# Four products of a constant tile on TensorE ahead of the first load, in a two-layer decoder kernel

## The chip, the cores and the metric

The kernel runs on one core of a Trainium2 chip. The metric is the time of one execution on the device in microseconds (us); lower is better. The inputs, weights and outputs are float32 and lie in the chip's memory; the core loads all of them itself at the start of each execution.

## The reference

The reference is a decoder with two layers over x of shape (8, 128, 128): 8 batches, 128 tokens, 128 channels. Each of six sub-blocks is added to its input and layer-normalised:

```
x = norm(x + gated_delta_rule(x))          # 16 heads of 8 channels, a scan over the tokens
x = norm(x + cross_attention(x, ctx))      # strided keys, 16 heads
x = norm(x + quantum_ffn(x))               # 128 -> 512 -> 128, with a sine in between
x = norm(x + selective_scan(x))            # 256 inner channels, 16 states, a scan over the tokens
x = norm(x + perceiver_attention(ctx, x))  # 8 heads of 128, keys from ctx and x
x = norm(x + receptance_ffn(x))
```

Only the head of the first sub-block matters for what follows. It is a projection and what hangs on it:

```
qkv   = x @ Wqkv.T                 # queries, keys, values
q, k  = q / |q|, k / |k|           # per head of 8 channels
alpha = sigmoid(x @ Wg.T + bg); beta = sigmoid(x @ Wb.T + bb)
S_t   = alpha (S - beta (S k) k') + beta v k'   # then o_t = S_t q_t
```

## The kernel before, in words

The kernel is one program written out by hand for the five engines. Each engine (TensorE, VectorE, ScalarE, GpSimd, and SyncE, which issues the DMAs) has its own block of instructions, runs them in the order in which they are written, and waits on named semaphores where it needs another engine's result. No scheduler moves anything. The output buffer of TensorE is one tile `ps` of eight banks with 512 columns each; `bank(k)` is the k-th.

SyncE issues eight loads right at the start (L374 to L381). The first, half of the pack `first`, holds the weights of the first projection, the gate biases and the first four batches of x, transposed; it raises `first_in`. The second holds the other four batches and the identity matrix and raises `second_in`. The context, the weights of later blocks and, last, the pack `late` (L381) follow.

TensorE begins with a wait for `first_in` (L1611). Then it multiplies each of the 8 batches with the weights of queries, keys, values and gates at once, 416 columns, into banks 0 to 7 (L1615). Each such float32 product is two weight loads and two matmuls in the trace, so L1615 stands there with 16 of each. ScalarE copies the even banks into the arena (L1174) and squares the queries and keys (L1170), VectorE copies the odd banks (L471) and squares the last batch (L477). TensorE then turns the gates (L1620), turns and sums the squares (L1628), and turns keys, queries and values (L1633). ScalarE applies the sigmoid (L1187) and the square root (L1190), VectorE the reciprocal (L501), and from there VectorE forms the small triangular systems and runs the scan over 32 chunks of 4 tokens (L566 to L581), with GpSimd and ScalarE beside it.

In later stages TensorE runs some products that nothing reads. The helper `stay_awake(n, k)` (L1597 to L1602) issues n products of the identity with 256 columns of the first weights into bank k. It can't be used before the first load has landed, since its operands come with that load.

ScalarE copies a small matrix out of the pack `late` (L1201) before it goes on with the folded weights of the second cross attention (L1204).

Of the kernel before, what the change touches and what calls it, by code (L numbers as in the profile page):

```python
# [18 lines left out]
P = 128  # L19
B, T, D = 8, 128, 128  # L20
# [62 lines left out]
def decoder(nc, first, x, early, context, fold, late, rows, out):  # L83
    with ExitStack() as ctx:
        sems = {}

        def S(name):
            name = RIDES[name][0] if name in RIDES else name
            if name not in sems:
                sems[name] = ctx.enter_context(nc.semaphore(name))  # L90
            return sems[name]
# [5 lines left out]
        def sb(name, shape, dt=F32):  # L97
            return ctx.enter_context(nc.sbuf_tensor(name, shape, dt))
# [40 lines left out]
        lat_mean = sb("lat_mean", [P, HB])  # L139
        cmean_rstd = sb("cmean_rstd", [P, B])  # L140
        table = sb("table", [P, 1])
        neg_a = sb("neg_a", [P, NH, NS])
        arena = sb("arena", [P, 27000])
        ps = ctx.enter_context(nc.psum_tensor("ps", [P, 8 * BANK], F32))
# [42 lines left out]
        def bank(k, n=1):  # L187
            return ps[:, k * BANK:(k + n) * BANK]
# [208 lines left out]
        def _(ve):  # L397
            count = [0]

            def step(ins):  # L400

                count[0] += 1
                ins.then_inc(S("vector_step"), 1)
# [62 lines left out]
                ve.wait_ge(S("normed"), normed(n, batches[-1] + 1))  # L466


            for b in range(1, B, 2):
                ve.wait_ge(S("qkv_mm"), b + 1)  # L470
                nc.vector.tensor_copy(qkvt[:, :, b], bank(b)[:, 0:3 * D + 2 * H].rearrange("p (n h) -> p n h", h=H)).then_inc(S("qkv_odd"), 1)  # L471
                if b == B - 3:
                    ve.wait_ge(S("ctx_in"), 16)
                    for i in range(2):
                        step(nc.vector.bn_stats(cstats[0:TC, i], kv_ctx[0:TC, i]))
# [1117 lines left out]
        def _(pe):  # L1593
            mm, turn = nc.tensor.matmul, nc.tensor.transpose
# [13 lines left out]
                    turn(turned_bank(n, g)[:, b % HB * T:(b % HB + 1) * T], xrow[:, n % 2, b], ident).then_inc(S("turned"), 1)  # L1608


            pe.wait_ge(S("first_in"), 16)  # L1611
            for b in range(B):
                if b == HB:
# [10 lines left out]
            for n in range(2):  # L1624
                if n:
                    pe.wait_ge(S("gates"), 2)
                for j in range(DH):
                    ins = mm(norm2[n], sq[:, (1 - n) * DH + j].rearrange("p b h -> p (b h)"), ident, is_transpose=True,  # L1628
                             start=(j == 0), stop=(j == DH - 1))
# [34 lines left out]
            for c in range(0, NC - NTAIL, 4):  # L1664
# [8 lines left out]
                for n, (pr, terms) in enumerate(((prod_s, DH), (prod_a, C))):  # L1673
                    pe.wait_ge(S("prods"), 2 * (c + n_c - 1) + n + 1)
                    for j in range(terms):
                        ins = mm(bank(6 + c // NR)[:, at:at + n_c * C * DH], ident,  # L1676
                                 pr[:, j, c % NR:c % NR + n_c].rearrange("p c t i -> p (c t i)"),
                                 start=(n == 0 and j == 0), stop=(n == 1 and j == terms - 1))
# [131 lines left out]
            for m in range(2):  # L1810
                pe.wait_ge(S("xcol"), 5 + m)
                for n in range(NH):
                    ins = mm(bank(4 + n)[:, 2 * m * T:2 * (m + 1) * T], W("w_in")[:, n * P:(n + 1) * P], xcol[:, 2 * m:2 * m + 2],
                             start=True, stop=True)
# [173 lines left out]
            for q in range(NQ):  # L1988
# [61 lines left out]
                if NK4 - 1 <= q < NK4 + 3:  # L2050
                    for h in range(2 * (q - NK4 + 1), 2 * (q - NK4 + 2)):
                        mm(bank(7)[:, h:h + 1], fk[:, h], W("bq1")[:, h:h + 1], start=(h == 0), stop=False)
                        last = mm(bank(7)[:, D:2 * D], W("bv1")[:, h:h + 1].to_broadcast([P, P]), fo[:, h],
                                  start=False, stop=(h == XH - 1))
# [149 lines left out]
```

## Time and profile before

| | |
|---|---|
| time, median of 3 runs | 368.13 us (367.89 to 369.22) |
| span of the profiled execution, first to last instruction | 365.6 us |
| what lies around the span (median less span) | 2.5 us |
| TensorE busy (matmul) | 314.8 us, 86% |
| VectorE busy | 301.9 us, 83% |
| ScalarE busy | 222.6 us, 61% |
| GpSimd busy | 201.8 us, 55% |
| mean granted TensorE clock | 0.957 |
| TensorE's wait for the first load | 4.1 us, once |

The profiled execution's own time is not given apart from its span, so the median stands beside it. In the rows, PE is TensorE's matmul, PEld its weight load, DVE is VectorE, ACT is ScalarE, POOL is GpSimd and SPq the queue of SyncE. Busy time is the time in which an engine executes; the brackets at the end of a row in order of time tell how long the engine sat idle before it and what ended this. The granted clock is 1.00 at 2.4 GHz and 0.50 at 1.2 GHz.

### The profile page before, as it was taken

How to read it: one execution, taken by the hardware profiler on the slowest of the kernel's cores; microseconds unless marked ns; L12 is line 12 of the kernel's file. 1: busy time of each engine (PE TensorE's matmuls, PEld its weight loads, DVE VectorE, ACT ScalarE, POOL GpSimd, SP SyncE). 2: the span in 40 equal slices, each digit the busy share in tenths (PEclk: the TensorE clock that was granted, in tenths of full speed). 3: DMA queues.
4: the chain of work that ended last, by engine and by line, in shares of the span. 5: the costliest groups of instructions: out<-in, count | busy, mean ns of one | idle time of the engine just before them, and what ended most of it. 6: DMA issues, size and time to landing. Idle time of an engine off the chain costs nothing. (4 is left out here: it accounts for less than half of the span.)

```text
span 365.6 us, 5686 instructions
## 1 busy us (share of the span) xinstructions
PE 314.8 (86%) x1758; PEld 239.0 (65%) x1758; DVE 301.9 (83%) x746; ACT 222.6 (61%) x515; POOL 201.8 (55%) x240
## 2 busy tenths in 40 slices
PE   5949396898998999868869989898799989999993
PEld 2647295686765647734436965576698668989873
DVE  0798999997988899999999999999949434754945
ACT  4666233334265869897777638888565656765742
POOL 2399996765504051899999999969503700100111
PEclk9978599899999999999996999999999999999997
DMA  8910000000000003345544534534100000000011
GB/s 257 417 63 2 1 0 3 0 1 2 0 2 1 0 2 119 121 138 161 148 130 114 186 104 146 160 126 139 64 2 0 2 1 0 3 0 2 1 30 29
DMA packets 11525, 24.45 MB, mean 67 GB/s; under 512 B 1231, under 2 KB 2255, under 8 KB 11239
## 3 DMA queue, kind: packets, MB, share of 16 engines
q1 hardware_dynamic: 11495, 24.09, 20.2%
q8 instruction: 14, 0.23, 0.3%
q14 instruction: 16, 0.13, 0.1%
HBM read 23.50 MB, written 0.59 MB: 66 GB/s over the span
## 5 line engine op out<-in xcount | busy, mean ns | idle before, releaser
L1101 POOL TENSOR_TENSOR arena<-arena 128x512 f32<-128x512 f32 x63 | 80.0, 1280 | 22.7 <-DVE arena L746 21.2
L746 DVE TENSOR_TENSOR_SCAN arena<-arena,ps 128x512 f32<-128x512 f32 x64 | 77.2, 1208 | 0.1
L1387 ACT ACTIVATE arena<-arena,neg_a 128x508 f32<-128x508 f32 x64 | 44.0, 717 | 6.9 <-DVE arena L746 5.9
L1863 PE MATMUL ps<-first_in,arena 128*128 128x128 f32 x256 | 41.0, 284 | 3.9 <-POOL arena L1101 3.7
L739 DVE TENSOR_TENSOR ps<-arena,ps 128x512 f32<-128x512 f32 x64 | 43.1, 676 | 0.1
L1147 POOL TENSOR_TENSOR rstd<-veps,mhalf 128x4 f32<-128x4 f32 (+2 forms) x6 | 5.0, 838 | 67.5 <-DVE veps L848 35.5
L1863 PEld LDWEIGHTS ps<-first_in,arena 128*128 128x128 f32 x256 | 32.3, 146 | 14.9 <-POOL arena L1101 8.3
L774 DVE TENSOR_REDUCE arena<-ps 128x2 f32<-128x496 f32 x32 | 21.3, 667 | 24.8 <-PE ps L1909 24.8
L1847 PE MATMUL ps<-arena,pick_wide 96*128 96x512 bf16 x64 | 25.2, 399 | 11.8 <-DVE arena L746 11.4
L1676 PE MATMUL ps<-arena,first_in 128*128 128x128 f32 (+1 forms) x192 | 26.2, 299 | 9.4 <-POOL arena L971 9.4
L1250 ACT ACTIVATE arena<-arena 128x64 f32<-128x64 f32 x31 | 12.9, 415 | 33.4 <-DVE arena L581 33.4
L1676 PEld LDWEIGHTS ps<-arena,first_in 128*128 128x128 f32 x192 | 25.2, 213 | 12.2 <-POOL arena L971 12.1
L1437 ACT ACTIVATE first_in<-ps 128x256 f32<-128x256 f32 x32 | 12.4, 386 | 30.8 <-PE ps L1935 30.5
L1423 ACT ACTIVATE arena<-ps,arena 128x248 f32<-128x248 f32 x64 | 29.4, 472 | 0.0
L971 POOL TENSOR_TENSOR arena<-arena 128x256 f32<-128x256 f32 x32 | 23.7, 742 | 8.3 <-DVE arena L581 8.0
L1602 PE MATMUL ps<-first_in 128*128 128x256 f32 x102 | 26.2, 391 | 2.2 <-ACT arena L1219 2.2
L1847 PEld LDWEIGHTS ps<-arena,pick_wide 96*128 96x128 bf16 x64 | 6.3, 98 | 28.6 <-DVE arena L746 25.8
L1909 PE MATMUL ps<-kvT,arena 128*128 128x248 f32 x96 | 24.1, 374 | 0.0
L1602 PEld LDWEIGHTS ps<-first_in 128*128 128x128 f32 x102 | 18.7, 197 | 5.8 <-ACT arena L1219 2.6
L1431 ACT ACTIVATE arena<-ps 128x512 f32<-128x512 f32 x32 | 19.2, 600 | 1.5 <-PE ps L1923 0.4
L1946 PEld LDWEIGHTS ps<-fold_vo,first_in 128*128 128x128 f32 x128 | 18.4, 191 | 1.8 <-ACT first_in L1437 0.5
L986 POOL TENSOR_TENSOR rstd<-veps,mhalf 128x2 f32<-128x2 f32 x8 | 5.7, 708 | 25.0 <-DVE veps L422 24.8
(302 smaller groups left out, 808.8 us busy)
## 6 DMA issues: line engine op xcount, KB each, us to landing
arena<-c_rows_dram SPq DMA_DIRECT2D x64, 256.0 KB, 3.2
fold_in<-in_fold_dram SPq DMA_DIRECT2D x1, 2056.0 KB, 11.2
late_in<-in_late_dram SPq DMA_DIRECT2D x1, 1423.5 KB, 17.2
early_in<-in_early_dram SPq DMA_DIRECT2D x1, 921.5 KB, 13.0
xres<-in_x_dram SPq DMA_DIRECT2D x1, 512.0 KB, 13.8
kv_ctx<-in_context_dram SPq DMA_DIRECT2D x1, 480.0 KB, 7.0
first_in<-in_first_dram SPq DMA_DIRECT2D x1, 465.0 KB, 3.4
rows_in<-in_rows_dram SPq DMA_DIRECT2D x1, 384.0 KB, 14.3
```

Of the source, the lines that this page charges most:

```text
L739: tt(chain(q), dtu[:, n, cols(g)], chain(q), ALU.mult).then_inc(S("drive"), 1)
L746: nc.vector.tensor_tensor_scan(hist[:, q % NBUF], fade[:, q % NFADE], chain(q), 0.0, ALU.mult, ALU.add).then_inc(S("scan"), 1)
L774: nc.vector.tensor_reduce(s5_max[:, u % 2], sim, AX.X, ALU.max, negate=True).then_inc(S("sim_max"), 1)
L971: tt(prod_s[:, :, c % NR].rearrange("p j t i -> p t i j"), Qg[:, c].unsqueeze(2).to_broadcast([P, C, DH, DH]), state[:, c].unsqueeze(1).to ...
L1101: tt(seen[:, q % NBUF], hist[:, q % NBUF], c_wide[:, q % NBUF], ALU.mult).then_inc(S("read_out"), 1)
L1387: act(fade[:, q % NFADE].rearrange("p (b t) -> p b t", t=T)[:, :, 1:], dt[:, n, cols(g)].rearrange("p (b t) -> p b t", t=T)[:, :, 1:], ACT ...
L1423: act(s5_p[:, u % 2, h], sim_bank(u)[:, h * 256:h * 256 + KV], ACT.Exp, bias=s5_max[:, u % 2, h:h + 1], accum_out=s5_den[:, u % 2, h:h + 1 ...
L1602: mm(bank(k)[:, 0:256], ident, W("w_qkvgb")[:, 0:256], start=True, stop=True)
L1676: ins = mm(bank(6 + c // NR)[:, at:at + n_c * C * DH], ident, pr[:, j, c % NR:c % NR + n_c].rearrange("p c t i -> p (c t i)"), start=(n == ...
L1847: mm(chain(q), pick[:, s], bc_parts[0:96, cols(g)], start=True, stop=True).then_inc(S("b_mm"), 1)
L1863: ins = mm(y_bank(p // NS)[:, b * T:(b + 1) * T], seen[:, p % NBUF, b * T:(b + 1) * T], ident, is_transpose=True, start=False, stop=last a ...
L1909: ins = mm(sim_bank(u)[:, i * 256:i * 256 + KV], s5_q[b // HB][h + i][:, b % HB * T:(b % HB + 1) * T], kvT[:, b], start=True, stop=True)
```

## The change

A tile `warm` of 128 x 256 float32 is added. VectorE fills it with 0.5 as its first instruction and raises the semaphore `warm`. TensorE waits for that semaphore before its wait for `first_in`, and multiplies the first 128 columns of the tile with all of its 256 columns, four times, into the first 256 columns of bank 7. Bank 7 is next written by the projection of batch 7, which starts its sum anew, so nothing reads the four products.

```diff
@@ tiles @@
         table = sb("table", [P, 1])
+        warm = sb("warm", [P, 256])
         neg_a = sb("neg_a", [P, NH, NS])
@@ VectorE's block @@
+            nc.vector.memset(warm[:], 0.5).then_inc(S("warm"), 1)
             for b in range(1, B, 2):
                 ve.wait_ge(S("qkv_mm"), b + 1)
@@ TensorE's block @@
+            pe.wait_ge(S("warm"), 1)
+            for _ in range(4):
+                mm(bank(B - 1)[:, 0:256], warm[:, 0:P], warm[:], start=True, stop=True)
             pe.wait_ge(S("first_in"), 16)
             for b in range(B):
                 if b == HB:
```

On TensorE, at the head of the program, the order before is this; `first_in` is the first pack, `arena` the working tile, and a float32 product stands as one row.

```order
L1592 UNCONDITIONAL_BRANCH
L1615 MATMUL ps<-first_in 128x416 x8
L1620 MATMUL ps<-first_in,arena 128x128 x2
L1628 MATMUL ps<-first_in,arena 128x128 x16
L1633 MATMUL ps<-first_in,arena 128x128 x24
```

The same place after the change:

```order
L1594 UNCONDITIONAL_BRANCH
L1615 MATMUL ps<-warm 128x256 x4
L1620 MATMUL ps<-first_in 128x416 x8
L1625 MATMUL ps<-first_in,arena 128x128 x2
L1633 MATMUL ps<-first_in,arena 128x128 x16
L1638 MATMUL ps<-first_in,arena 128x128 x24
```

Four products stand ahead of the projection, which is now L1620; all else keeps its order. On VectorE, at the head of its block, before:

```order
L396 UNCONDITIONAL_BRANCH
L471 COPY arena<-ps 128x26x16 x3
L475 BN_STATS cstats<-kv_ctx 120x6 x2
L471 COPY arena<-ps 128x26x16
L477 TENSOR_TENSOR arena<-arena 128x16x16
```

and after the change:

```order
L397 UNCONDITIONAL_BRANCH
L470 MEMSET warm 128x256
L473 COPY arena<-ps 128x26x16 x3
L477 BN_STATS cstats<-kv_ctx 120x6 x2
L473 COPY arena<-ps 128x26x16
L479 TENSOR_TENSOR arena<-arena 128x16x16
```

The fill stands ahead of the first copy out of the projection. ScalarE, GpSimd and SyncE run what they ran.

## Rows read from the trace of the kernel before

**Rows 1.** The page, lines 2 and 4: 40 equal slices of the span; the last chain.

```profile
PEclk9978599899999999999996999999999999999997
...
PE 25%; DVE 1%; ACT 1%; issue 1%; POOL 1%; POOLq 0%; DVEq 0%
```

**Rows 2.** Instructions in time: start us, us, engine, instruction, idle before it.

```profile
0.73 1.28 ACT L1174 ACT_TABLE_LOAD   x1 [0.73 <-PEq L2193]
0.73 0.52 POOL L907 MEMSET arena<- 128x512 f32 x1 [0.29 <-POOLq L2193]
0.74 0.38 SPq L374 DMA_DIRECT2D first_in<-in_first_dram  x1
...
4.14 8.72 PE L1615 MATMUL ps<-first_in 128*128 128x416 f32 x16 [4.14 <-DMA first_in<-in_first_dram]
```

**Rows 3.** TensorE's weight loads of the first projection, same columns.

```profile
9.16 0.34 PEld L1615 LDWEIGHTS ps<-first_in 128*128 128x128 f32 x1 [0.36 <-issue]
9.85 0.24 PEld L1615 LDWEIGHTS ps<-first_in 128*128 128x128 f32 x1 [0.36 <-issue]
10.25 0.19 PEld L1615 LDWEIGHTS ps<-first_in 128*128 128x128 f32 x1 [0.16 <-issue]
```

**Rows 4.** Stretches: width, busy PE, PEld, DVE, ACT, POOL (count), PEclk, DMA share, GB/s.

```profile
5.00:6.00 1.00, 1.00 (x3) 0.64 (x2) 0.00 (x0) 0.06 (x1) 0.00 (x0) 1.00 1.33 340
...
23.00:24.00 1.00, 1.00 (x10) 1.00 (x9) 1.00 (x2) 1.00 (x1) 1.00 (x2) 0.80 0.00 0
```

**Rows 5.** Keep-awake products (L1602), at either clock level, in time.

```profile
38.05 2.07 PE L1602 MATMUL ps<-first_in 128*128 128x256 f32 x4 [2.15 <-ACT arena L1219]
...
48.54 1.03 PE L1602 MATMUL ps<-first_in 128*128 128x256 f32 x4
```

**Rows 6.** ScalarE, VectorE and TensorE around the first projection's end, in time.

```profile
5.94 0.52 ACT L1174 ACTIVATE arena<-ps 128x416 f32<-128x416 f32 x1 [3.92 <-PE ps L1615]
...
6.47 1.28 ACT L1159 ACT_TABLE_LOAD   x1
...
12.61 1.02 ACT L1170 ACTIVATE arena<-arena 128x256 f32<-128x256 f32 x3
12.90 0.59 DVE L471 COPY arena<-ps 128x416 f32<-128x416 f32 x1 [0.41 <-PE ps L1615]
13.53 0.42 DVE L477 TENSOR_TENSOR arena<-arena 128x256 f32<-128x256 f32 x1
...
14.08 0.63 ACT L1187 ACTIVATE arena<-ps,first_in 128x128 f32<-128x128 f32 x2 [0.45 <-PE ps L1620]
14.10 1.94 PE L1628 MATMUL ps<-first_in,arena 128*128 128x128 f32 x16
14.73 1.28 ACT L1190 ACT_TABLE_LOAD   x1
...
16.36 0.95 DVE L501 RECIPROCAL arena<-ps 128x128 f32<-128x128 f32 x1
```

**Rows 7.** The first load of constants for late stages, and ScalarE's use of it.

```profile
4.01 1.12 SPq L381 DMA_DIRECT2D late_in<-in_late_dram  x1
...
22.60 1.89 ACT L1201 ACTIVATE pick_wide<-late_in 96x2048 bf16<-96x2048 f32 x1
22.65 2.68 PE L1643 MATMUL ps<-fold_in 128*128 128x128 f32 x15 [4.00 <-DVE arena L512]
```

**Rows 8.** DMA issues of the page: size, us from issue to landing.

```profile
late_in<-in_late_dram SPq DMA_DIRECT2D x1, 1423.5 KB, 17.2
```

**Rows 9.** Later stretches; columns as in rows 4.

```profile
16.00:85.00 69.00, 52.47 (x309) 45.93 (x307) 67.20 (x272) 29.53 (x91) 58.39 (x82) 0.85 0.06 24
...
87.00:90.00 3.00, 1.96 (x16) 1.64 (x16) 1.36 (x4) 0.76 (x3) 1.22 (x6) 1.00 0.02 5
...
189.00:192.00 3.00, 2.02 (x10) 1.38 (x10) 3.00 (x5) 2.99 (x5) 2.88 (x3) 0.81 0.51 154
192.00:195.00 3.00, 2.50 (x10) 1.44 (x9) 3.00 (x5) 2.97 (x5) 2.67 (x3) 0.50 0.50 159
```

## The prediction

> **What bounds the kernel now.** I began with the page's clock line and its last chain [rows 1]. The chain is TensorE's in the last quarter of the span; before that it changes hands. The clock line has low digits in slices 3 to 5 and one in slice 22, and none in the first slice. The change is at the very start, so what counts is whether time won there reaches the end.
>
> Next I read the first microseconds in order of time [rows 2]. ScalarE, GpSimd and SyncE are let go at 0.73 to 0.74 us. TensorE does nothing until the first load lands at 4.14, so 3.4 us of it are free.
>
> Then I looked at how fast the projection ran. The clock column grants 1.00 at 5 to 6 us, and says 0.80 and less only from 23 us on [rows 4]. The durations say otherwise: a weight load takes 0.34 us at 9.16 and 0.19 at 10.25, and they stand 0.69 us apart (9.16 to 9.85) before the turn and 0.35 after it (the same 416 columns at twice the pace) [rows 3]. Before about 9.9 us TensorE ran at 1.2 GHz, after it at 2.4, and the column shows this only from its first recorded change on. The rise came 5.7 us after its first product (9.85 less 4.14). In the first 5.7 us eight of the 16 matmuls ran at half rate.
>
> The Trainium skill ("TensorE: Matmul & The Clock Gate", Part 1: The HAM clock gate) says that an idle array is held at 1.2 GHz by default and activity releases it. By that rule, the durations agree and the column does not.
>
> Who waits for the projection: VectorE and ScalarE stand idle for it, the last copy begins at 12.90 after 0.41 us of idling, and the turn of the gates, the sigmoid at 14.08, the table load at 14.73 and the reciprocal at 16.36 follow link by link [rows 6]. From 16 to 85 us VectorE is busy 67.20 of 69.00 us [rows 9]: the span there is its work, which starts when that chain lets it. So a shift at 16.36 moves the whole scan with it.
>
> **The change part by part.**
>
> *The fill.* No fill by VectorE stands in the trace. GpSimd fills 512 columns in 0.52 us [rows 2]; VectorE's product over 256 columns takes 0.42 [rows 6]. Bounds are 0.1 and 0.5 us; I take 0.3, nearest to half of the first. VectorE has nothing else to do then, so it costs nothing there. The step from VectorE to TensorE is 0.15 us (its last square ends at 13.53 + 0.42 = 13.95, TensorE begins at 14.10 [rows 6]). The block so begins at 0.74 + 0.3 + 0.15 = 1.2 us, between 1.0 and 1.4.
>
> *The four products.* They are 8 matmuls of 256 columns. At the low clock one takes 0.69 x 256/416 = 0.43 us, eight 3.4 us. The keep-awake products, which have this shape, agree on the ratio: four matmuls take 2.07 us at the low clock and 1.03 at the high one, tails and first load included [rows 5]. So the block ends at 1.2 + 3.4 = 4.6 us, 0.5 after the load has landed. It costs 0.5 us (between 0.3 and 0.7), unless the clock rises inside it.
>
> *The clock.* If it rises 5.7 us after the first product again, it rises at 6.9 us instead of 9.9. Projection before: 8.2 matmuls at 0.69 and 7.8 at 0.35, from 4.14 to about 12.6. Projection after, from 4.6: 2.3 us at the low clock are 3.3 matmuls, 12.7 follow at 0.35, that is 4.4 us, end at about 11.35. It ends 12.6 - 11.35, some 1.2 us earlier.
>
> *What is late next.* ScalarE: its first copy starts 1.80 us after the first matmul [rows 2, 6], so at 6.4. From there it has four copies of 0.52, a table load of 1.28 with 0.2 behind it, and seven squares of some 0.35 (1.02 for three): 6.0 us without a gap. It is through at 12.45, where it was through at 13.63 [rows 6]: 1.2 us earlier. VectorE's last square (13.95 before) comes at 12.7. TensorE's next stage starts behind the later of the two, at about 12.9 instead of 14.10. So 1.2 us are kept, and ScalarE has no slack left: any larger gain of TensorE would be cut to about what ScalarE lets through.
>
> *Loads.* `late` lands 17.2 us after its issue at 4.01, that is at 21.2 [rows 7, 8]. ScalarE uses it at 22.60, now at 21.4. It still does not wait, with 0.2 us to spare.
>
> *Sum.* 1.2 us off the profiled span of 365.6, so 364.4; with the 2.5 us between the span and the median of the runs, 366.9 us. As the profile is one execution and the runs differ by 1.3 us among themselves, I let the profiled execution stand for the median. Bounds of the unknown terms, start of the block and fill, move this by 0.2 us either way. Bounds of the rise are wider: not before 4.1 us (all of the projection at the high clock) and, at the latest, where it was.
>
> The same section of the Trainium skill says that the moment of the rise against the start of a kernel varies from run to run, and advises against fitting to one count of slow products. By that rule the 1.2 us are one draw among several; one profile can't show it here, so it goes into the spread only, and the middle stays at the row's 5.7 us.
>
> **The rivals.**
>
> *Nothing is won (368.0 to 368.4).* Either the rise stays at 9.9 us since these constants do not bring it on, or TensorE was at its high clock as the column says. In the first case the projection starts 0.5 us late and still meets the rise at 9.9: half of the 0.5 us is lost, +0.25, 368.4. In the second, the block takes 8 x 0.21 = 1.7 us, ends at 2.9 before the load, and the time is 368.1. For the second speaks only the column; against it the durations [rows 3, 4]. For the first speaks nothing but that no product of constants stands in the trace. A gain that a later wait swallows would give the same time; VectorE's 97% from 16 to 85 us speaks against it.
>
> *More than forecast (365.8).* The clock rises before or near the first load. Then the projection takes 16 x 0.35 = 5.6 us from 4.14 and ends at 9.8, 2.8 us earlier. ScalarE's 6.0 us from about 5.3 end at 11.3, 2.3 us earlier, and that is the cap: 365.8. Its table matrix would wait for `late` at 20.3 to 21.2, ahead of work that VectorE needs only at 32 us. Speaks for it: TensorE is active 2.9 us sooner; against it: the only rise measured at the start took 5.7 us of full work.
>
> *Slower (370).* Everything behind 16 us is moved against the moments at which the clock changes. The trace has it fall at about 191 us, when TensorE had been busy 2.02 of 3 us, and at 192 to 195 it stands at 0.50 [rows 9]. There VectorE was busy 3.00 of 3 and nothing was lost. At 87 to 90 us TensorE is busy only 1.96 of 3, VectorE and ScalarE even less, and the clock held at 1.00 [rows 9]. If it falls there in the moved timing, some 6 us of TensorE's work (one low slice or so, as at 192) run at half rate in a stage that waits for it: about +3 us, less the 1.2 won, 370. It decides from the point at which more than 2.4 us of such work lie on the path. In the profile all low stretches lie beside a busy VectorE, so this is a small chance.
>
> **How the numbers follow.** About 0.5% (1.8 us) is what a measurement of this kernel can tell from no change. Forecast: 366.9, 0.53. Nothing won: 0.23. More: 0.17. Slower: 0.07. The forecast itself lies within 0.5%. Faster by over 0.5%, below 366.3: three quarters of the third case and a sixth of the first, 0.22. Slower by over 0.5%, above 370.0: 0.05, as half of the last case and some spread. Same: 0.73. The range goes from the third case's time, less some, 365.5, to beyond the second's, 368.7. The forecast's own range is 366.2 to 367.6.
>
> **What would show it.** A fill on VectorE of 0.2 to 0.4 us at about 0.75; the first of 8 matmuls at about 1.2, half of them or more 0.43 us apart; the first weight load of 0.19 us near 7 us, where it was near 10; the reciprocal (16.36 before) near 15.2; and the same shift at 85 us and at the end. A rise at 9.9 shows the first rival, a projection all at 0.35 us the second. Wrong would be the forecast if the reciprocal moved by 1.2 us and the end did not, or if the block began after 2 us.

## The result: 365.06 us, 0.72% faster, outside the predicted range

| | median | lowest, highest | runs |
|---|---|---|---|
| before, beside it | 368.13 us | 367.89, 369.22 | 4 |
| changed | 365.06 us | 364.95, 365.21 | 4 |

The ratio is 0.9928, with a 95% interval of 0.9909 to 0.9946. The gain is 3.1 us in the medians, where 1.2 were forecast and the range ended at 365.5.

The page of the changed kernel, its clock line and its last chain, which answer to [rows 1]:

```profile
PEclk9968599899999999989987989999999999999997
...
PE 25%; DVE 1%; ACT 1%; issue 1%; POOL 1%; POOLq 0%; DVEq 0%
```

The chain is the same. The clock line has three more low digits in the middle (slices 18, 21 and 24, each at 8, beside slice 22); what one such stretch does is told below.

The head of the changed kernel in order of time (start us, us, engine, instruction, idle before it), answering to [rows 2, 3, 6, 7]:

```profile
0.86 0.27 DVE L470 MEMSET warm<- 128x256 f32 x1 [0.86 <-PEq L2198]
...
1.19 3.46 PE L1615 MATMUL ps<-warm 128*128 128x256 f32 x8 [1.19 <-DVE warm L470]
...
4.58 0.30 PEld L1620 LDWEIGHTS ps<-first_in 128*128 128x128 f32 x2 [0.34 <-DMA first_in<-in_first_dram]
4.58 5.85 PE L1620 MATMUL ps<-first_in 128*128 128x416 f32 x16
5.04 0.19 PEld L1620 LDWEIGHTS ps<-first_in 128*128 128x128 f32 x1 [0.16 <-issue]
...
10.19 1.02 ACT L1172 ACTIVATE arena<-arena 128x256 f32<-128x256 f32 x3
...
11.67 1.94 PE L1633 MATMUL ps<-first_in,arena 128*128 128x128 f32 x16
...
13.93 0.95 DVE L503 RECIPROCAL arena<-ps 128x128 f32<-128x128 f32 x1
...
21.25 1.91 ACT L1203 ACTIVATE pick_wide<-late_in 96x2048 bf16<-96x2048 f32 x1 [1.03 <-DMA late_in<-in_late_dram]
```

The fill, the start at 1.19 and the block of 3.46 us are near the forecast. What differs is the clock. The projection's weight loads take 0.19 us from its head on, so all of it runs at 2.4 GHz. The rise lies inside the block already: where the whole block ran at the low clock (e1 below) the same eight matmuls took 3.78 us. The packed trace also keeps the moments at which the clock changed; the first one kept is 9.95 us in the trace of before, where its weight loads turn, and 4.18 us here. This first moment is called the rise from here on. Its 16 matmuls end at 10.43, where they ended at 12.86, and the reciprocal starts 2.43 us earlier, not 1.2.

The whole span is 2.4 us shorter (365.6 to 363.2). Set against each other at six places of VectorE's stream:

| VectorE, start of | before | changed | this stretch gives |
|---|---|---|---|
| first reciprocal | 16.36 | 13.93 | +2.43 |
| first small reduction of the scan (L571, now L573) | 34.42 | 31.56 | +0.43 |
| last small reduction of the scan | 84.66 | 81.44 | +0.36 |
| middle of the second scan | 199.80 | 196.55 | +0.03 |
| last step of the second scan | 261.48 | 259.12 | -0.89 |
| last instruction | 361.98 | 359.62 | 0.00 |

Three things stand in this table: the head (2.43), 0.79 us that nobody asked for between 16 and 85 us, and 0.89 us lost near 220 us.

The 0.79 us are two pauses of VectorE. In the kernel before:

```profile
34.42 0.51 DVE L571 TENSOR_REDUCE arena<-arena 128x16 f32<-128x144 f32 x2 [0.33 <-ACT arena L1246]
...
77.15 0.55 DVE L581 TENSOR_REDUCE arena<-arena 128x32 f32<-128x160 f32 x2 [0.26 <-DVE arena L576]
```

and the same two places after the change:

```profile
31.56 0.50 DVE L573 TENSOR_REDUCE arena<-arena 128x16 f32<-128x144 f32 x2
...
73.93 0.53 DVE L583 TENSOR_REDUCE arena<-arena 128x32 f32<-128x160 f32 x2
```

The brackets with 0.33 and 0.26 us of idling are gone. The names in them are inferred releasers. In the changed kernel the first reduction starts before ScalarE's L1248 (31.64), the line named for it before, so this was not what held it.

The loss near 220 us, after the change:

```profile
219.16 0.70 DVE L741 TENSOR_TENSOR ps<-arena,ps 128x512 f32<-128x512 f32 x1 [0.77 <-PE ps L1852]
```

and its stretch (width, busy PE, PEld, DVE, ACT, POOL, granted clock, DMA share, GB/s):

```profile
216.00:219.00 3.00, 3.00 (x8) 1.33 (x7) 2.39 (x3) 2.83 (x7) 2.63 (x3) 0.50 0.61 143
```

The clock stood at 0.50 there, TensorE was late with L1852, and VectorE waited 0.77 us. In the trace before, that stretch ran at 1.00.

Last, the changed execution took 365.03 us with a span of 363.2: 1.8 us around the span, and 1.8 to 1.9 in every later trace. I had taken 2.5. By that the profiled execution of before took some 365.6 + 1.8 = 367.4 us (an estimate), 0.7 less than its median. So of the 3.1 us between the medians, 2.4 stand between the two traces, and 0.7 are the distance of the profiled execution from the median before.

### The profile page after: what moved, and what is told of

Read it like the earlier page. It is cut to its first block and busy times, and to the rows that moved or that the text cites. A ratio compares the mean times of both kernels' runs of the same rounds, so it can differ in the third digit from the quotient of the medians.

```text
span 363.2 us, 5703 instructions
## 1 busy us (share of the span) xinstructions
PE 317.6 (87%) x1766; PEld 242.1 (67%) x1766; DVE 302.0 (83%) x747; ACT 222.4 (61%) x515; POOL 201.6 (56%) x240
## 5 line engine op out<-in xcount | busy, mean ns | idle before, releaser
L1868 PE MATMUL ps<-first_in,arena 128*128 128x128 f32 x256 | 42.2, 290 | 3.1 <-POOL arena L1103 2.8
L1868 PEld LDWEIGHTS ps<-first_in,arena 128*128 128x128 f32 x256 | 33.4, 149 | 14.5 <-POOL arena L1103 7.7
L1852 PE MATMUL ps<-arena,pick_wide 96*128 96x512 bf16 x64 | 25.8, 408 | 11.7 <-DVE arena L748 11.3
L1852 PEld LDWEIGHTS ps<-arena,pick_wide 96*128 96x128 bf16 x64 | 6.4, 100 | 28.5 <-DVE arena L748 24.9
```

The lines of the kernel that those rows point to most:

```text
L1852: mm(chain(q), pick[:, s], bc_parts[0:96, cols(g)], start=True, stop=True).then_inc(S("b_mm"), 1)
L1868: ins = mm(y_bank(p // NS)[:, b * T:(b + 1) * T], seen[:, p % NBUF, b * T:(b + 1) * T], ident, is_transpose=True, start=False, stop=last a ...
```

## The experiments

In the edits, `...` and `mm(...)` stand for arguments that are left out. Minus lines are those of the changed kernel; e14 to e16 add to the kernel before.

Theory A: the clock rises a fixed time after TensorE's first product. Theory B: the moment of the rise is drawn anew in each execution, and the block moves the whole draw. Theory C, formed when traces of other kernels showed the same two steps of the table (+0.43 and +0.36): one more instruction at VectorE's head removes two pauses. Medians stand beside those of the kernel before in the same batch: 368.03 for e1 to e4, 367.89 for e5 to e8, 367.84 for e9 to e12, 367.83 for e13 to e16, 367.52 for e17 and e18.

**e1, the changed kernel again** (no edit).

> The changed kernel once more, beside the kernel before. Theory A (the clock is up by the first load's product whenever TensorE begins 3 us sooner): 365.0 to 365.3 us, again 2.5 to 3 us under the kernel before, the first 0.19 us weight load at the head of the projection, the reciprocal near 13.9. Theory B (the early rise was one lucky draw of a rise that varies from run to run): the times spread by 1 us and more, and in this trace the first short weight load stands somewhere in the middle of the projection, so the reciprocal comes between 13.9 and 15.5.

365.99 us (365.48 to 366.36), ratio 0.9948 (0.9935 to 0.9962). Its trace (same columns) has the first short load 2.3 us later than the first one, and the rise at 7.03 us, 2.8 us later:

```profile
1.18 3.78 PE L1615 MATMUL ps<-warm 128*128 128x256 f32 x8 [1.18 <-DVE warm L470]
...
7.29 0.19 PEld L1620 LDWEIGHTS ps<-first_in 128*128 128x128 f32 x1 [0.16 <-issue]
...
15.13 0.95 DVE L503 RECIPROCAL arena<-ps 128x128 f32<-128x128 f32 x1
```

The same program, block from 1.18 us on as in the first trace, and the reciprocal 1.2 us later. Theory A is out. The median lies 0.9 us over that of the first four runs.

**e2 and e9, waiting only.** VectorE fills eleven times, TensorE waits for the last.

```diff
-            nc.vector.memset(warm[:], 0.5).then_inc(S("warm"), 1)
+            for k in range(11):
+                if k:
+                    ve.wait_ge(S("warm"), k)
+                nc.vector.memset(warm[:], 0.5).then_inc(S("warm"), 1)
-            pe.wait_ge(S("warm"), 1)
-            for _ in range(4): mm(...)
+            pe.wait_ge(S("warm"), 11)
```

> No products; VectorE fills the tile eleven times, one after the other, and TensorE waits for the last, at about 4.6 us, so the projection starts as late as with the block. Theory A (the products raise the clock): the projection begins at half rate, the rise comes at 9 to 11 us, and the time is 0 to 0.5 us over the kernel before, 368.1 to 368.7. Rival (it is not the products but VectorE's early work, or where the projection now lies): the time stays at 365 to 366.

> The kernel that only waits for eleven fills, once more. Its first runs fell into two groups, 366.8 to 367.4 and 368.6 to 369.2 us, and its trace was of the slower one, with a rise at 11.2. Theory B (rise drawn per execution): a trace of the faster group shows a rise at 7.5 to 8.5 us although no product stood ahead of the projection, and the two groups differ by half of what their rises differ. Rival (the fills themselves help in the faster group): the trace has the rise at 9 us or later and the time is under 367.5 all the same.

367.01 us (366.75 to 369.20) and 367.25 (366.82 to 368.48): ratios 0.9990 and 0.9991, both intervals holding 1. Without products most of the gain is gone. The first trace:

```profile
5.10 0.50 PEld L1621 LDWEIGHTS ps<-first_in 128*128 128x128 f32 x2 [5.10 <-DVE warm L473]
...
11.37 0.19 PEld L1621 LDWEIGHTS ps<-first_in 128*128 128x128 f32 x1 [0.22 <-issue]
```

The second has its rise at 8.98, its first short load at 9.21, and took 367.27 us. I had expected 7.5 to 8.5; this is what the rival had said (9 or later and still under 367.5). The medians lie 0.6 to 1.0 us under the kernel before although the projection starts at 5.10. That was the first sign of Theory C: these kernels too have instructions at VectorE's head.

**e3, zeros.** The tile is filled with 0.0.

```diff
-            nc.vector.memset(warm[:], 0.5).then_inc(S("warm"), 1)
+            nc.vector.memset(warm[:], 0.0).then_inc(S("warm"), 1)
```

> The tile is filled with 0.0 in place of 0.5, nothing else. Theory A (it counts that TensorE works, whatever the values): 365.1 us, projection at the high clock as in the changed kernel. [...]

365.08 us (364.80 to 366.22), rise at 5.69, first short load at 5.92, reciprocal at 14.47. That is early, as with 0.5: whether the tile holds 0.0 or 0.5 does not count here.

**e4 and e6, three and two products** (`range(3)`, `range(2)`).

> Three products in place of four: the block ends at 1.2 + 2.6 = 3.8 us, before the load lands, so the projection starts at 4.14 in place of 4.6. Theory A1 (the clock still rises at 4 to 4.6 us): 0.4 us less than the changed kernel, 364.7. Theory A2 (the gap of 0.4 us between block and projection puts the rise off): the first matmuls of the projection run at half rate, rise between 6 and 8 us, the time 0.5 to 1.5 us over the changed kernel, 365.6 to 366.6.

> Two products: the block ends at 2.9 us and TensorE sits idle for 1.2 to 1.7 us until the load. Theory B with the idle time counted against it: the rise is as late as without the block, 7 to 11 us, and the time is the kernel before's, 367.5 to 368.5. Rival (any early activity brings the rise forward by as much as the first product comes earlier): the time is near that of four products, 365.0 to 366.4.

Three: 365.33 us, but 364.33 to 368.10; three of ten runs were over 366.5. The trace of its slowest run:

```profile
1.19 2.93 PE L1615 MATMUL ps<-warm 128*128 128x256 f32 x6 [1.19 <-DVE warm L470]
4.60 1.76 PE L1620 MATMUL ps<-first_in 128*128 128x416 f32 x2 [0.49 <-DMA first_in<-in_first_dram]
...
10.86 0.19 PEld L1620 LDWEIGHTS ps<-first_in 128*128 128x128 f32 x1 [0.21 <-issue]
```

TensorE sat idle for 0.49 us between block and projection, and the rise came as late as without a block, at 10.71. Two products: 367.25 us, five runs at 366.3 to 366.8 and five at 367.7 to 368.5, rise at 8.04. The median lies 0.6 us under the kernel before, no more than two pauses that are gone in it (below), so this block brought nothing that shows. The best run of three products (364.33) is no better than the best of four over all batches (364.11), and a block that ends before the load is a gamble: three of ten runs and five of ten were late, none of the 15 runs of the changed kernel was over 366.4. That the gap itself is the cause is argued from these counts; one trace shows it. (The first load took 3.4 us from issue to landing in the traces of before and of e1, and 3.5 to 4.0 in all others. So the fourth product mostly cost less than the 0.5 us of the forecast.)

**e5, the kernel before again.**

> The kernel before once more. Theory B (the moment of the rise is drawn anew in each execution, and the time follows it by half a microsecond per microsecond): the runs spread over 1.5 to 2 us around 368.0, and the trace shows the first short weight load somewhere between 7 and 11 us; time and rise lie on one line with the other traces, 365.0 at a rise of 4.6 and 368.6 at 11.3. Theory A (the rise comes a fixed 5.7 us after the first product): 9.9 us again.

367.97 us, spread 366.89 to 368.58. Its trace has the rise at 7.33 us:

```profile
7.32 0.20 PEld L1615 LDWEIGHTS ps<-first_in 128*128 128x128 f32 x1 [0.36 <-issue]
```

and the reciprocal at 15.18, not 16.36: the rise I had built on (9.9) was one draw, and a late one.

**e7, late start.** Four fills in a row, so the block starts at 2.36.

> VectorE fills the tile four times, so the block starts at about 2.3 in place of 1.2 us and ends near 5.7, if at the low clock; all else as in the changed kernel. If the gain is the head start of TensorE, 1.1 us of it go, and the projection starts 1.1 us later: 366.2 to 367.3, rise between 5 and 8.6 us. If only the count of products mattered, the clock would be up at the block's end: 366.0.

366.57 us, ratio 0.9965 (0.9952 to 0.9978), rise at 6.73, first short load at 7.03. It is 1.3 us under the kernel before, where the changed kernel is 2.0 to 3.1 under it: about half of the gain goes with 1.2 us of the head start.

**e8 and e12, a constant of one column** with four and five products, no fill.

```diff
-            nc.vector.memset(warm[:], 0.5).then_inc(S("warm"), 1)
-            pe.wait_ge(S("warm"), 1)
+            ones = [nc.const_aps.tensor(1.0, [P, n], F32) for n in (P, 256)]
-                mm(bank(B - 1)[:, 0:256], warm[:, 0:P], warm[:], ...)
+                mm(bank(B - 1)[:, 0:256], ones[0], ones[1], ...)
```

> No tile and no fill: the four products read a constant of one column, repeated, that every program of this kind holds from its start, so they begin at about 0.9 in place of 1.19 us. The head start grows by 0.3 us: rise 0.3 us earlier on average, time 0.15 to 0.3 us under the changed kernel, 365.2 as median, lowest near 364.6. If the block ended before the load by more than 0.3 us, runs with a late rise (367 and more) would appear among them.

> The constant of one column in place of the tile, and five products: the block starts at 0.78 and ends at 5.0 us at the low clock, so no gap is left before the load (4.1 to 4.7). Compared with four products of the tile, rise 0.4 us earlier on average, projection up to 0.3 us later where the rise comes late: 365.0 to 365.6 as median, none over 366.6. With four products of the constant the gap of 0.3 to 0.7 us before the load may have put off the rise in some executions (median 366.1); if so this one is faster than that.

366.12 and 366.09 us. Both start at 0.78 us. Both were expected to be faster than the changed kernel; their medians lie over the 365.99 of e1, the slower of its batches so far, and e12 has two runs over the 366.6 that it was to stay under. In e12 the reciprocal starts at 14.42, early as hoped, but the span is 364.5: both kernels have the two pauses, 0.8 us, since VectorE has no fill at its head (below).

**e10 and e11, fill only and six products.**

> One fill of the tile by VectorE, no product and no wait on TensorE. All theories: no difference from the kernel before, 367.9 within 0.3 us, spread 366.7 to 369. A median under 367 would mean that the tile or the fill brings something by itself.

> Six products: the block lasts from 1.2 to 6.3 us at the low clock, less where the rise comes inside it. The rise is drawn as with four (4.2 to 7.4), every execution has it by about 7.4, and the projection starts 0.7 to 1.7 us later. Theory: 0.5 to 1.2 us over the changed kernel, median 366.1 to 366.8. Rival (a longer block makes the rise come earlier or more surely): 365.0 to 365.5 and a narrower spread.

Six: 366.28 us, as expected; the projection starts at 6.47, and the rise stands at 7.01. The fill alone: 366.64 us (365.87 to 368.86), ratio 0.9975 (0.9959 to 0.9990), where all theories said no difference. Measured by stretches of VectorE's stream, the traces fell into two kinds, whatever TensorE's clock did:

| first reciprocal to first small reduction | first to last small reduction | kernels |
|---|---|---|
| 18.03 to 18.06 us | 50.24 to 50.25 us | before, e5, e8, e12 |
| 17.63 to 17.68 us | 49.87 to 49.90 us, e7 50.07 | changed, e1, e2, e3, e4, e6, e7, e9, e10, e11 |

e8 and e12 hold the tile in memory as well but do not fill it, so it is not the tile's place. What the second kind shares is an instruction at VectorE's head. The next four runs test this.

**e13, GpSimd fills the tile** (the fill stands first in GpSimd's block; four products).

> Four products of the tile as in the changed kernel, but GpSimd fills it, as the first instruction of its block, so VectorE's stream is that of the kernel before. Theory C (0.76 us of the gain come from VectorE having one more instruction at its head: two pauses of 0.33 and 0.26 us that it shows before its L571 at 34.4 and its L581 at 77.2 are gone): both pauses are back, the stretch from VectorE's first reciprocal to its last small reduction of the scan is 68.3 us and not 67.5, and the median is 366.0 to 366.8. Rival (the products alone give it all): 67.5 us, median 365.0 to 365.9.

365.64 us (364.63 to 366.54). The stretches are 18.06 and 50.25 us, and the pause is back:

```profile
32.15 0.51 DVE L572 TENSOR_REDUCE arena<-arena 128x16 f32<-128x144 f32 x2 [0.32 <-ACT arena L1248]
```

So the stretches came out as Theory C put them, and the median did not: it is in the rival's range and better than Theory C's 366.0 to 366.8. With both pauses in place, the products alone were worth 2.2 us in this batch. The rise of its trace, at 4.50, is an early one.

**e14, e15, e16: a one-column fill** and no products, at VectorE's head, in the 17th chunk of its scan, and behind the scan. The tile is allocated in all three.

```diff
+            nc.vector.memset(warm[:, 0:1], 0.5)
```

> The kernel before with one fill of a single column by VectorE at the head of its block, 0.1 us, nothing else. Theory C (one instruction more is what counts, not what it does): no pause, 67.5 us from reciprocal to last small reduction, median 367.0 to 367.3, 0.7 us under the kernel before. Rival (the size of the fill, or chance): 68.3 us and 367.9.

> The one-column fill stands in the 17th of the 32 chunks of VectorE's scan, between the places of the two pauses. Theory C (the place in the stream decides): the first pause stays (reciprocal to first small reduction 18.05 us), the second goes (first to last small reduction 49.9 us, plus up to 0.15 for the fill itself), median 367.5. Rival (anything early in the program): both go, or none.

> The one-column fill stands behind the scan, and the tile is allocated. Theory C: both pauses stay, 18.05 and 50.24 us, 367.9. Rival (the tile's kilobyte, which moves the arena, is what counts): both are gone, 367.1.

| fill | first stretch | second stretch | median us |
|---|---|---|---|
| head (e14) | 17.63 | 49.88 | 367.29 |
| 17th chunk (e15) | 18.05 | 49.90 | 367.35 |
| behind the scan (e16) | 18.06 | 50.23 | 367.92 |

In e15 the first pause stands and the second is gone:

```profile
33.96 0.51 DVE L574 TENSOR_REDUCE arena<-arena 128x16 f32<-128x144 f32 x2 [0.31 <-ACT arena L1249]
```

All six stretches came out as Theory C put them. The medians agree (0.5, 0.5 and -0.1 us against before), but their intervals hold 1, so the traces carry this, not the times. That the pauses reach the end shows over all traces: from the first reciprocal to the end of the span the 13 traces without pauses take 349.1 us on average, the six with both 349.8.

**e17 and e18, the changed kernel once more, and both gains in their smallest form** (e8 with the one-column fill at VectorE's head).

> The changed kernel a third time, as the measure for the next. Both theories: 365.0 to 366.4 us, median 365.6, no pause on VectorE (67.5 us from reciprocal to last small reduction).

> Both gains in their cheapest form: four products of the one-column constant, from 0.78 us on, and a one-column fill by VectorE at its head. Theory: no pause (67.5 us), rise 0.4 us earlier than in the changed kernel on average but, in some runs, put off by the gap before the load; median 365.1 to 365.6, 0.8 us under the same kernel without the fill (366.12), at best 0.2 us under the changed kernel.

364.43 us (364.11 to 365.31), ratio 0.9920 (0.9903 to 0.9938), and 365.00 (364.72 to 366.11), ratio 0.9939 (0.9923 to 0.9956). The small form has no pause (17.65 and 49.89 us) and its reciprocal is at 13.91, but it does not beat the change: 0.6 us over it in the same batch. The two traces show why these two executions differ. The rise of e18 stands at 3.87, but the projection can't start before the load lands, at 4.55, so the sooner start had nothing left to give; and VectorE waits 0.70 us for L1852 at 219 us, the loss of the first trace again, which e17 does not have. Whether its other runs have that loss isn't known. No version here beats the change. e17's trace shows what the change is worth without the loss at 220 us:

```profile
216.00:219.00 3.00, 2.73 (x13) 1.47 (x12) 3.00 (x5) 3.00 (x7) 2.65 (x3) 1.00 0.52 143
```

Here the clock held at 1.00 and VectorE was busy throughout. The reciprocal is at 13.85, hardly earlier than in the first trace, but the span is 362.4, 0.8 less.

Six of these executions, with their own times, show how the rise carries through:

| trace | projection starts | first 0.19 us load | reciprocal | time us |
|---|---|---|---|---|
| e17 | 4.60 | 4.96 | 13.85 | 364.23 |
| changed | 4.58 | 5.04 | 13.93 | 365.03 |
| e3 | 4.76 | 5.92 | 14.47 | 365.20 |
| e1 | 4.76 | 7.29 | 15.13 | 366.18 |
| e4 | 4.60 | 10.86 | 16.97 | 368.10 |
| e2 | 5.10 | 11.37 | 17.48 | 368.64 |

All six have no pause. From top to bottom the first short load moves 6.4 us, the reciprocal 3.6, the time 4.4; 0.9 of the last is the loss at 220 us, which e4 and e2 have as well (62.6 against 61.7 us in that stretch).

## Why the prediction was wrong

*The bound and the path* were right: the 3.4 us of waiting were free, the projection was at 1.2 GHz in spite of the clock column, and what it gains at the reciprocal reaches the end. (One slip in the clock line: slice 8, at 8, is low as well.)

*The fill and the block* were right in place (1.19 us). The length of 3.46 us fits the forecast of 3.4 partly by luck: at the low clock throughout it is 3.78 (e1), and here the clock rose inside it. Their cost of 0.5 us was too high, since the load mostly lands later than in the one trace: the projection starts at 4.52 us on average in the six traces named below without products, and at 4.69 in the five with them.

*The clock* is the step that failed. The forecast let the rise come 5.7 us after the first product, as in its one trace, so at 6.9 us in place of 9.9, and priced that at 1.2 us. Counted from TensorE's first product, the rise came after 2.9 to 6.2 us (4.8 on average) in the eight traces without products ahead, and after 3.0 to 6.2 us (4.4 on average) in the ten with a block that no gap parts from the projection. So the delay has the same spread with and without the block, as Theory B says, and 5.7 is near its late end. I had the spread named, put it into the range only, and kept the middle at a single late draw. In the five traces with four products of the tile (changed, e1, e3, e13, e17) the rise stands at 5.2 us on average, in the six without products and without a delay (before, e5, e10, e14, e15, e16) at 9.2: it moves by 4.0 us and not by 3.0. The reciprocal starts at 14.29 in the former and at 16.18 in the latter. The term is 1.9 us, not 1.2, and in the compared pair it was 2.43, an early draw against a rather late one. The case "more than forecast" had the mechanism and, with 2.3 us at the reciprocal, nearly the size. Its cap by ScalarE did not bind (squares done at 11.21) and ScalarE's wait for `late`, 1.03 us, cost nothing, as it said.

*"It costs nothing there"*, said of the fill, was wrong in its sign, and this term of the sum was missing. The fill on VectorE brings 0.79 us by two pauses that go. Nothing in my reading looked at the brackets of VectorE at 34 and 77 us, which lie in the 1.8 of 69.00 us that were read as "its work"; the second names VectorE as its own releaser, which should have been suspect.

*The time around the span* was 1.8 us and not 2.5. The 0.7 us between the two is how much faster the profiled execution of before was than its median. The prediction let the one stand for the other, and the predicted median came out 0.7 too high.

*The slower rival* happened in small: a low stretch of the clock in the moved timing met VectorE at 219 us and took 0.8 to 0.9 us. It did not decide.

Together, for the compared pair: 366.9 less 0.7 (around the span), less 1.2 (clock), less 0.8 (pauses), plus 0.9 (220 us) is 365.1; measured 365.06.

How much of this is the draw: three batches of the changed kernel lie 3.1, 2.0 (e1) and 3.1 us (e17) under the kernel before, and the middle one, 365.99 us, would have been inside the predicted range. The average terms, 1.9 and 0.8, give 2.7 us, that is 365.4 us from 368.13 (an estimate), just outside it.

What stays open is what the pauses are; where they stand can be told. They are 42.7 us apart (34.42 to 77.15). Counted in the packed trace, with the entries for its waits, the two paused reductions are the 64th and the 320th entry of VectorE's stream, 256 apart, in all six traces with both pauses. With one or eleven instructions more at its head, the 320th entry is a wait for a semaphore, and nothing pauses there; with one, the 64th is such a wait too. In e15 the 64th is a reduction and pauses, the 320th is a wait and does not. With four more (e7) the 320th is a reduction again, and it does pause, in small: the pair takes 0.68 us, where its neighbours take 0.50, and this is the 50.07 in the table.

```profile
74.78 0.68 DVE L576 TENSOR_REDUCE arena<-arena 128x16 f32<-128x144 f32 x2
```

The 64th entry of e7, a reduction behind a wait of VectorE, and that of e2 and e9, among instructions of 0.4 us and more, show no pause. The Trainium skill ("Runtime: NRT & Kernel Launch", Instruction fetch mechanics) says that an engine's instructions are fetched in blocks of 256 and that crossing into the next is mostly hidden. The distance of 256 agrees with it. A block's edge that falls where VectorE has no wait to hide it would look like this, but no run here shows a fetch, so this cause is argued and not shown. Open too is why TensorE's clock fell near 216 us in some executions and not in others.

## What to carry to other kernels

Where a program waits for its first load, let TensorE multiply anything it can reach, and let the block last until the load lands: a shorter one loses the head start in some executions. Where a term hangs on the moment at which the clock rises, take several traces, or the spread of the times, before it is priced. A gain of a few tenths of a per cent may come from the added instruction rather than from what it does; run the instruction alone.

## What the runs showed of the hardware

- The rise of the clock is not tied to the first product: it stood at 4.18 and 7.03 us in two traces of one program with the same start (changed, e1). Over 18 traces it came 2.9 to 6.2 us after the first product of unbroken work.
- Products of zeros brought an early rise like those of 0.5 (5.69 us, 365.08 us).
- The granted clock reads 1.00 before the first recorded change, while weight loads of 0.34 us show the low level.
- An idle gap of 0.49 us ahead of the projection went with a rise at 10.71 us (e4), in a run of 368.10 us; seven of its ten runs took 364.3 to 365.5.
- VectorE paused for 0.33 and 0.26 us at the 64th and the 320th entry of its stream, and one instruction more at its head, of 0.06 us, removed both (e14).
